# A graph attention layer: edge attributes turned by VectorE instead of TensorE, four buffers per stage instead of two, and edge lists read whole and turned into tables

## The reference, cut to what matters

```python
Q, K, V = x @ Wq + bq, x @ Wk + bk, x @ Wv + bv      # (12500, 96) each
E = edge_attr @ We + be                              # (412500, 96)
score = K[src] * Q[dst] / sqrt(12) * E               # per edge
score = exp(clip(score.reshape(-1, 8, 12).sum(-1), -5, 5))
wV = segment_sum(V[src] * score, dst)                # per destination node
Z  = segment_sum(score, dst)
out = layernorm(x + wV / (Z + 1e-6))
```

## Time and profile before

| what | value |
|---|---|
| median of 3 runs | 5354.8 us (5341.96 to 5366.8) |
| the profiled execution | 5346.04 us, its span 5344.1 us |
| TensorE's granted clock, mean | 0.508 |
| until VectorE's first product in the loop | 135.9 us |
| from VectorE's last such product (5253.25) to the end | 91 us |
| DMA packets | 497,769, 607.5 MB |

### The profile page before, as it was taken

One profiled execution on the slowest core, in us unless ns is written; L12 is line 12 of the kernel. 1 busy time (PEld: TensorE's weight loads), 2 busy tenths in 40 slices (PEclk: granted clock), 3 DMA queues, 4 the chain that ended last, 5 costly groups with the idle time before them and its releaser, 6 DMA issues.

```text
span 5344.1 us, 72613 instructions
## 1 busy us (share of the span) xinstructions
PE 3563.7 (67%) x19972; PEld 3430.0 (64%) x19973; DVE 2070.6 (39%) x6072; ACT 1676.7 (31%) x3477; POOL 3154.1 (59%) x3274
## 2 busy tenths in 40 slices
PE   7666666666666666666666666666666666666665
PEld 6666666666666666666666666666666666666664
DVE  4433333333333333333333343333333333333336
ACT  4323232333323332323332332333322323333234
POOL 4566565565665656555656566655566565665662
PEclk7555555555555555555555555555555555555555
DMA  7344444444444444444444444444444444444443
GB/s 227 107 110 118 110 109 109 109 118 110 109 111 113 115 109 110 118 110 108 110 113 113 109 108 110 114 113 109 109 110 119 108 112 112 114 109 108 110 117 91
DMA packets 497769, 607.51 MB, mean 114 GB/s; under 512 B 256053, under 2 KB 420224, under 8 KB 497630
## 3 DMA queue, kind: packets, MB, share of 16 engines
q0 software_dynamic: 155200, 318.39, 22.6%
q1 hardware_dynamic: 233215, 281.36, 18.0%
q10 hardware_dynamic: 109330, 7.48, 1.5%
HBM read 584.51 MB, written 22.46 MB: 114 GB/s over the span
## 4 chain that ended last, share of the span: by engine, by line
PE 46%; issue 25%; another core or an unknown queue 18%; DVE 6%; DVEq 2%; ACT 1%; DMA 1%; SPq 1%; ACTq 0%; POOL 0%; POOLq 0%
PE bank L637 16%; PE bank L651 15%; PE bank L635 10%; PE bank L644 4%; DVE kqe L906 2%; DVE raw_score L917 1%; DVEq L298 1%; DVE oh L901 1%; DVE kqe L898 0%; ACT eaT L767 0%; DMA out_dram<-spare 0%; ACT spare L805 0%; DVE msg L910 0%; DVE accT L925 0%
## 5 line engine op out<-in xcount | busy, mean ns | idle before, releaser
L527 POOL DMA_INDIRECT kv<-kv_table,src_idx x3224 | 3104.5, 963 | 2090.2 <-DVE msg L910 1041.2
L637 PE MATMUL bank<-w_e,eaT 97*128 97x96 f32 x6448 | 1882.9, 392 | 216.6 <-issue 216.6
L635 PE MATMUL bank<-ident,ea 128*96 128x128 f32 x3224 | 1355.3, 421 | 958.3 <-issue 517.5
L637 PEld LDWEIGHTS bank<-w_e,eaT 97*128 97x128 f32 x6448 | 1776.7, 334 | 222.8 <-issue 221.9
L898 DVE TENSOR_TENSOR kqe<-kv,bank 128x384 f32<-128x384 f32 x806 | 446.6, 554 | 3179.6 <-remote 2432.5
L651 PE MATMUL bank<-oh,msg 128*104 128x32 f32 x6448 | 1284.8, 353 | 276.7 <-issue 273.5
L635 PEld LDWEIGHTS bank<-ident,ea 128*96 128x96 f32 x3224 | 806.0, 250 | 986.2 <-issue 515.0
L651 PEld LDWEIGHTS bank<-oh,msg 128*104 128x104 f32 x6448 | 1234.3, 289 | 269.0 <-issue 264.9
L764 ACT ACTIVATE msg<-score 128x32 f32<-128x32 f32 x806 | 184.8, 229 | 3523.9 <-remote 2569.5
L644 PEld LDWEIGHTS bank<-q_win,ohT 96*128 96x128 bf16 x3224 | 401.4, 155 | 338.8 <-issue 332.4
L644 PE MATMUL bank<-q_win,ohT 96*128 96x96 bf16 x3224 | 447.2, 279 | 245.5 <-issue 241.1
(11 more groups left out here) (78 smaller groups left out, 481.0 us busy)
## 6 DMA issues: line engine op xcount, KB each, us to landing
ea<-in_edge_attr_dram SPq DMA_DIRECT2D x201, 768.0 KB
dst_b<-dst_by_chunk SPq DMA_DIRECT2D x201, 384.0 KB
kv<-kv_table,src_idx POOLq DMA_INDIRECT x3224
q_win<-q_table SPq DMA_DIRECT2D x806, 19.9 KB
kv_table<-kv_out SPq DMA_DIRECT2D x25, 336.0 KB
q_table<-q_out SPq DMA_DIRECT2D x25, 252.0 KB
spare<-in_x_dram SPq DMA_DIRECT2D x25, 168.0 KB
out_dram<-spare SPq DMA_DIRECT2D x25, 168.0 KB
```

The costliest lines, as they stand in the source:

```text
L527: pool.indirect_dma_start(kv[:, slot, g, :], None, kv_dram[:, :], bass.IndirectOffsetOnAxis(ap=src_idx[:, u, g:g + 1], axis=0)).then_inc(k ...
L635: last = nc.tensor.transpose(eaT_ps[u % 2][0:D, g * P:(g + 1) * P], ea[:, u, g, :], ident[:, :])
L637: nc.tensor.matmul(e_ps[v % 2][:, g * D:(g + 1) * D], eaT[:, v % 2, g * P:(g + 1) * P], w_e[:, :], start=True, stop=True)
```

## The change

The attributes are loaded already cut into blocks of 32 features: partition i of a block holds feature values of edges i, i+32, ... in runs of 32 floats, so that a transpose of 32x32 blocks by VectorE gives the layout that TensorE needs, features on partitions and edges along the row. TensorE turns nothing in the loop any more, and ScalarE copies nothing. The ring of loaded attributes has 16 slots of one chunk, loaded four at a time, three DMAs each, from ScalarE's queue (the first 16 from SyncE's). The PSUM banks freed by this give four buffers each of `e_ps` with `sum_ps` (which share a bank) and `q_ps`; `eaT`, `ohT`, `oh` and `msg` have four too. VectorE turns, and ScalarE builds `ohT`, four chunks ahead (`lead=DEPTH`). TensorE's step s projects chunk s, and VectorE's step a waits for TensorE's step a. The accumulation into `accT` comes five chunks late instead of three.

The edges of a chunk lie in another order (edge g*128+p at partition p, group g). The source list is read whole, made float, turned by TensorE and kept as a table, like the destinations; ScalarE copies four chunks of it at a time into `src_idx` as integers. Both lists are loaded by GpSimd instead of ScalarE. Their turning is spread over node batches 9 to 22. The inputs x are loaded by SyncE instead of ScalarE. Every second piece of `accT` is cleared by ScalarE. `x_in`, `kv_out`, `q_out` and `dst16` share memory with the loop's rings. The destination loads of the loop move from SyncE's queue to ScalarE's. The second pass is adapted in the same way.

```diff
-PROJ_LAG = 2
 SUM_LAG = 5
+DEPTH = 4
+TURN_DST = 9
+SQ = 32
 SEL = WIN * PARTS
 SEL_READ = 106
 RING = 8
 HALF = RING // 2
+EA_RING = 16
+EA_GROUP = 4
+EA_AHEAD = EA_RING - 1
...
+    for s in range(-lead, unroll):
+        step(s, s % unroll, None)
...
+        kv_mem = sb("kv_mem", [P, RING * G * 2 * D])
+        kv = kv_mem[:, :].rearrange("p (c g d) -> p c g d", g=G, d=2 * D)
+        x_in = kv_mem[:, 0:4 * BATCH * D].rearrange("p (u j d) -> p u j d", j=BATCH, d=D)
+        kv_out = kv_mem[:, 4 * BATCH * D:12 * BATCH * D].rearrange("p (u j d) -> p u j d", j=BATCH, d=2 * D)
+        ea_mem = sb("ea_mem", [P, EA_RING * CHUNK])
+        ea = ea_mem[0:D, :].rearrange("p (c e) -> p c e", e=CHUNK)
+        src_nat = ea_mem[0:NQ, 0:NJ * CHUNK]
+        dst16 = ea_mem[0:NQ, NJ * CHUNK:NJ * CHUNK * 3 // 2].bitcast(I16)
+        q_out = ea_mem[:, NJ * CHUNK * 3 // 2:NJ * CHUNK * 3 // 2 + 2 * BATCH * PARTS * D].bitcast(BF16).rearrange(
+            "p (u j k d) -> p u j k d", j=BATCH, k=PARTS, d=D)
...
-        eaT = sb("eaT", [DA, 2, CHUNK])
+        eaT = sb("eaT", [DA, DEPTH, CHUNK])
         away = sb("away", [SEL, CHUNK], BF16)
-        ohT = sb("ohT", [SEL, 2, CHUNK], BF16)
-        oh = sb("oh", [P, 2, G, WIN])
+        ohT = sb("ohT", [SEL, DEPTH, CHUNK], BF16)
+        oh = sb("oh", [P, DEPTH, G, WIN])
...
-        msg = sb("msg", [P, 2, G, DZ])
+        msg = sb("msg", [P, DEPTH, G, DZ])
...
-        eaT_ps, e_ps, q_ps, sum_ps = bank[0:2], bank[2:4], bank[4:6], bank[6:8]
+        e_ps = [bank[i][:, 0:G * D] for i in range(DEPTH)]
+        sum_ps = [bank[i][0:DZ, G * D:G * D + WIN] for i in range(DEPTH)]
+        q_ps = bank[DEPTH:2 * DEPTH]
...
+        def load_edges(engine, s, g):
+            count = min(EA_GROUP, C - s) if isinstance(s, int) else EA_GROUP
             whole = count - 1 if isinstance(s, int) and s + count == C else count
-            if whole > 0:
-                engine.dma_start(src_idx[:, u:u + whole, :], src[bass.ds(s * CHUNK, whole * CHUNK)].rearrange(
-                    "(c p g) -> p c g", p=P, g=G)).then_inc(src_idx_in[u // IDX_GROUP], 16)
-            if whole < count:
-                engine.dma_start(src_idx[:, u + whole, :], src[E - CHUNK:E].rearrange(
-                    "(p g) -> p g", g=G)).then_inc(src_idx_in[u // IDX_GROUP], 16)
+            parts = [(s * CHUNK, g * EA_GROUP, whole)] + ([(E - CHUNK, g * EA_GROUP + whole, 1)] if whole < count else [])
+            for edge, slot, chunks in parts:
+                for k in range(0, D, SQ):
+                    engine.dma_start(ea[k:k + SQ, slot:slot + chunks, :].rearrange("i c (b f) -> i (c b) f", f=SQ),
+                                     edge_attr[bass.ds(edge, chunks * CHUNK), k:k + SQ].rearrange(
+                                         "(b i) f -> i b f", i=SQ)).then_inc(ea_in[g], 16)
+        def landed_edges(engine, c, u):
+            if isinstance(c, int):
+                last = c // EA_GROUP == (C - 1) // EA_GROUP
+                engine.wait_ge(ea_in[u // EA_GROUP], 16 * (D // SQ) * (c // EA_RING + (2 if last else 1)))
+            else:
+                engine.wait_ge(ea_in[u // EA_GROUP], (c - u) * (16 * (D // SQ) // EA_RING) + 16 * (D // SQ))
...
+                if not isinstance(b, int) or 4 <= b < BATCHES:
+                    sp.wait_ge(x_turned, b - 3)
+                    load_x(sp, b, u)
+                if not isinstance(b, int) or b >= 3:
+                    m, um = b - 3, (u - 3) % 4
+                    sp.wait_ge(kv_evac, (m + 1) * 2)
+                    for lo, hi in NODE_PARTS:
+                        sp.dma_start(kv_t[lo:hi, bass.ds(m * BATCH, BATCH), :], kv_out[lo:hi, um, :, :]).then_inc(kv_stored[um], 16)
...
-                sp.wait_ge(pe_step, s - HALF + PROJ_LAG)
+                sp.wait_ge(pe_step, s - HALF)
                 sp.sem_inc(loads_allowed, 1)
-                load_edges(s, h)
-                load_destinations(s, h)
...
+            sp.wait_ge(src_turned, NJ)
+            load_edges(sp, 0, 0)
+            sp.wait_ge(dst16_stored, 32)
+            load_edges(sp, EA_GROUP, 1)
             for h in range(2):
-                load_edges(h * HALF, h)
-            sp.wait_ge(dst16_stored, 32)
-            for h in range(2):
-                load_destinations(h * HALF, h)
+                load_destinations(sp, h * HALF, h)
...
+            for g in range(2, EA_RING // EA_GROUP):
+                load_edges(sp, g * EA_GROUP, g)
...
+            for lo, hi in ((0, NP16), (NP16, NQ)):
+                pool.dma_start(dst_nat[lo:hi, :].bitcast(I32), dst[lo * NJ * CHUNK:hi * NJ * CHUNK].rearrange(
+                    "(q r) -> q r", q=hi - lo)).then_inc(dst_in, 16)
+            pool.dma_start(dst_end_row[:, :], dst[E - CHUNK:E].rearrange("(a r) -> a r", a=1)).then_inc(ends_in, 16)
+            pool.dma_start(dst_end[:, :], dst[E - CHUNK:E].rearrange("(g p) -> p g", g=G), allow_slow_non_contiguous=True).then_inc(ends_in, 16)
+            for lo, hi in ((0, NP16), (NP16, NQ)):
+                pool.dma_start(src_nat[lo:hi, :].bitcast(I32), src[lo * NJ * CHUNK:hi * NJ * CHUNK].rearrange(
+                    "(q r) -> q r", q=hi - lo)).then_inc(src_in, 16)
+            pool.dma_start(src_end[:, :], src[E - CHUNK:E].rearrange("(g p) -> p g", g=G), allow_slow_non_contiguous=True).then_inc(src_end_in, 16)
...
+            pool.wait_ge(src_in, 32)
+            nc.gpsimd.tensor_copy(src_nat, src_nat.bitcast(I32)).then_inc(src_float, 1)
...
+                j = b - TURN_DST
+                if 0 <= j < NJ:
+                    pe.wait_ge(dst_float, 1)
+                    at_least(pe, rel_made, j)
+                    turn(j, dst_nat, bank[6], dst_turned)
+                elif NJ <= j < 2 * NJ:
+                    pe.wait_ge(src_float, 1)
+                    pe.wait_ge(src_made, j - NJ + 1)
+                    turn(j - NJ, src_nat, bank[7], src_turned)
...
+                n, v, w = s - SUM_LAG, u % DEPTH, (u - SUM_LAG) % DEPTH
+                projecting = not isinstance(s, int) or s < C
+                summing = not isinstance(s, int) or n >= 0
                 if projecting:
-                    pe.wait_ge(eaT_copied, c + 1)
-                    at_least(pe, kqe_done, c - 1)
-                for g in range(G):
-                    if turning:
-                        last = nc.tensor.transpose(eaT_ps[u % 2][0:D, g * P:(g + 1) * P], ea[:, u, g, :], ident[:, :])
-                    if projecting:
-                        nc.tensor.matmul(e_ps[v % 2][:, g * D:(g + 1) * D], eaT[:, v % 2, g * P:(g + 1) * P],
+                    pe.wait_ge(ea_turned, s + 1)
+                    for g in range(G):
+                        nc.tensor.matmul(e_ps[v][:, g * D:(g + 1) * D], eaT[:, v, g * P:(g + 1) * P],
                                          w_e[:, :], start=True, stop=True)
-                if projecting:
-                    pe.wait_ge(ohT_built, c + 1)
-                    landed(pe, q_win_in, c, v, 16)
-                    sel = ohT[:, v % 2, :].rearrange("n (p g) -> n g p", g=G)
+                    pe.wait_ge(ohT_built, s + 1)
+                    landed(pe, q_win_in, s, u, 16)
                     for g in range(G):
-                        last = nc.tensor.matmul(q_ps[v % 2][:, g * D:(g + 1) * D], sel[:, g, :], q_win[0:SEL, v, :],
+                        last = nc.tensor.matmul(q_ps[v][:, g * D:(g + 1) * D], ohT[:, v, g * P:(g + 1) * P], q_win[0:SEL, u, :],
                                                 start=(g == 0), stop=(g == G - 1), skip_group_check=True)
+                else:
+                    pe.wait_ge(acc_added, n - DEPTH + 1)
+                    pe.wait_ge(msg_ready, n + 1)
                 if summing:
-                    pe.wait_ge(msg_ready, n + 1)
-                    pe.wait_ge(oh_built, n + 1)
-                    at_least(pe, acc_added, n - 1)
                     for g in range(G):
-                        last = nc.tensor.matmul(sum_ps[w % 2][0:DZ, 0:WIN], msg[:, w % 2, g, :], oh[:, w % 2, g, :],
-                                                start=(g == 0), stop=(g == G - 1))
+                        last = nc.tensor.matmul(sum_ps[v], msg[:, w, g, :], oh[:, w, g, :],
+                                                start=(g == 0), stop=(g == G - 1), skip_group_check=True)
                 last.then_inc(pe_step, 1)
...
+            def copy_sources(s, u):
+                count = max(0, min(IDX_GROUP, C - s)) if isinstance(s, int) else IDX_GROUP
+                if count > 0:
+                    nc.scalar.copy(src_idx[:, u:u + count, :], src_tab[:, bass.ds(s * G, count * G)].rearrange(
+                        "p (c g) -> p c g", g=G)).then_inc(src_copied, count)
...
+                    if u % 2 == 1:
+                        nc.scalar.copy(accT[:, bass.ds(b * (BATCH * NP), BATCH * NP)],
+                                       zero[:, 0:1].to_broadcast((P, BATCH * NP))).then_inc(acc_zeroed, 1)
...
-                c, v = s - 3, (u - 3) % RING
```

(57 more changed lines are left out.)

178 lines of the change are left out of this document (73 added, 105 removed).

## The result

| | kernel before | changed kernel |
|---|---|---|
| median | 5360.8 us (5341.96 to 5368.18, 4 runs) | 5302.79 us (5293.67 to 5312.92, 4 runs) |
| ratio | | 0.9898, 95% interval 0.9865 to 0.9931 |
| span of the profiled execution | 5344.1 us | 5300.4 us |

The forecast was 4,455 us, in a range of 4,250 to 5,200. The kernel became 1.0% faster, and the large term, the removal of 1,000 us of waits, did not come.

The account below looks back on a forecast made before the run. Gathers were taken as the floor, with some 1,000 us of waits from late TensorE signals. 141 + 10, 798 chunks x 5.20 = 4,150, 3, 91 and 50 for remaining waits, plus run offsets, gave 4,455 us, range 4,250 to 5,200.

Parts of the forecast that it names:

- the large term: Loop buffers, two to four: GpSimd never runs out of free gather buffers, so 1,000 us of waits go.
- table making: Before the loop: cast, turns, copies and moved loads delay the first free gather buffer by 10 us, ends -10 and +30.
- floor of 5.01 us: Loop: four gathers a chunk, 1.25 us from start to start, are the floor; 806 chunks give 4,038 us.
- rival 1: Loop: late signals end only when gathers pause, so longer bursts still end in 4.8 us pauses; 5,050 us, chance 0.27.
- Rival 4: Loop buffers do nothing, since signals are late by as much as buffers are deep; 5,300 to 5,400 us, chance 0.05.
- Rivals 2 and 3: Short attribute runs fill the DMA engines, 6,800 us, chance 0.06; issuing loads holds ScalarE, 6,300 us, chance 0.07.
- Transpose: VectorE gains one 96x512 transpose a chunk, 0.73 us, or 1.45 at half rate; hidden behind the gathers.
- Short runs: Attribute loads in 128-byte runs: 1.24 million packets at 14.5 ns, 17.9 ms of DMA engine time, hidden.
- ScalarE's issues: ScalarE's queue issues attribute and destination loads: 1.5 to 8 us per four chunks, hidden at 1.34 us each.
- VectorE beside the gathers: Gathers issued beside VectorE's products take 1.14 instead of 0.95 us; one in four gives 5.20 us a chunk.
- TensorE: Loop: TensorE loses four transposes a step, 4.05 to 3.50 us, both under 5.01, worth nothing by itself.

Follow-up runs that it names:

- late kind: Comparisons (series timed together) in which the unchanged kernel before took 5,361, 5,441, 5,511 and 5,326 us.
- e16: Changed kernel, loop in five stretches: gathers of 128, 64, 16 rows; plain DMAs; two of each. 4502.85 us; 6.4 us a chunk with gathers, 3.5 plain, 3.7 mixed.
- e1: Changed kernel with two buffers per stage instead of four and sums three chunks late instead of five: 5505.43 us, 1.012 of the kernel before.
- e4: Changed kernel with attributes loaded in runs of 2,048 bytes instead of 128, values in another order: 0.9856 of the kernel before.
- prompt kind: Comparisons (series timed together) in which the unchanged kernel before took 4,249, 4,260, 4,253 and 4,250 us.
- e2: Changed kernel with two gathers a chunk instead of four after the first eight chunks, half the sources left out: 3153.79 us, 3.60 us a chunk.
- e9: Changed kernel again, without an edit, beside the kernel before: 4312.28 us, 1.0124 of the kernel before.
- e10: Kernel before again, unchanged, with its profile: 4251.22 us.
- e13: Changed kernel with the x loads given back to ScalarE from SyncE: 4293.42 us, 1.0097 of the kernel before.
- e17: Changed kernel, loop in five stretches with GpSimd clearing 0, 1, 96, 192, 320 scratch columns behind each gather: 5245.01 us; 6.29, 6.34, 6.31, 6.24, 6.10 us a chunk.
- e12: Changed kernel with two buffers per stage instead of four, the edit of e1: 4317.92 us, 1.0135 of the kernel before.

## Why the prediction was wrong

**The step that failed** is the sentence "If signals come late no matter whether the gathers pause, GpSimd never runs out of free buffers and the 1,000 us of waits go." That the counts come late was read rightly. I took the lateness for a delay of fixed length, ten us, that a pause of the gathers does not change, and set four buffers of 20 us against it. The runs show that the count on which the next gathers depend comes with the pause: 3.1 us after the start of a burst's last gather before and 3.6 us after, and its lag grew with the burst, from 9.7 to 14.3 us. VectorE's waits for it stayed at 2,500 us. With four free buffers GpSimd gathers four chunks and then stands, as it stood after three or four before. The gathers of the late kind keep to a rate, 1.53 to 1.64 us each over whole loops and long stretches (1.60 before, 1.57 after), whatever their rows (e16) and however many buffers there are (e1). Depth does not bridge that. The loop takes 6.38 us a chunk before and 6.30 after, instead of 5.20. By 798 chunks the missing 1.10 us are some 875 us; the sum had allowed 50 of them, and the table making took 21 more than forecast, which together is the whole error of 848 us.

**What could have been read.** The floor of 5.01 us was taken from the shortest distance of the gathers in the earlier trace rows. The same rows give 19.73 us for a period of twelve. The row with one product and 0.92 us behind "issue", and the 1,229 us of such rows shown above, already had TensorE itself stalled. And the two microseconds between the last gather and the count were in the prediction, under rival 1.

**The rivals.** Rival 1, at a chance of 0.27, had the mechanism: late signals that end only when the gathers pause, and longer bursts that each end in a pause (5.07 us, 4.8 forecast). It let five or six chunks go by in a burst where four did, and so came to 5.8 to 6.2 us a chunk instead of 6.3. Rival 4 had the time (5,300 to 5,400) at a chance of 0.05, and half of the reason, for the lag did grow with the buffers; that they do nothing is off by the 2.2% of e1. Rivals 2 and 3 did not occur.

**The sum, term by term.** *Transpose:* 0.70 us, 0.73 taken. *Short runs:* 1.245 million packets, 1.24 forecast, and 16 x 5,300 x 0.235 by 1,245,734 is 16.0 ns each, 14.5 forecast; hidden, as e4 shows. The Trainium skill, page "DMA: Bandwidth & Descriptors", section "Specifications", asks for 512 bytes at least; by my line of two means 33 ns would have been the price of such a packet, an estimate. The trace does not bear that estimate out: 16.0 ns on the mean. *ScalarE's issues:* three attribute loads hold it 3.22 us at 3012.28; hidden. *VectorE beside the gathers:* 5.20 us a chunk taken, 5.08 where nothing else is in the way, of which the change added 0.04. *TensorE:* 3.50 us taken, 3.52 to 3.60 in e16 and e2. *Table making:* +10 forecast, +30.7 in the result (171.7 against 141.0) and +23.4 in e9 against e10. I had counted the attribute loads that pass SyncE's query stores but not the x loads: they lay in ScalarE's queue before, and in SyncE's they stand between the stores of every node batch. That is 13.4 us (e13). The remaining 10, to which the turning of both lists and the attribute loads belong, were not split further.

**The account of the result.** To the last gather 38.8 us less (5,195.0 against 5,233.8), and 4.9 less behind it: together the 43.7 us of the two spans. The loop from first freed buffer to last gather gained 69.5 and the table making gave back 30.7. In the prompt kind the loop has nothing to gain, loses 31.8 to slower gathers, and the table making 23.4 more.

**What stays open.** What it is that gathers, TensorE's and SyncE's instructions and the counts share was not found; that it is one thing is the simplest reading of e16 and e17, not shown. Whether it acts by a rate or by a least distance between gathers is open too: e17 fits neither alone. Nor is it known what makes a comparison late or prompt: neither the kernel nor its inputs differ. It is not the chip alone: the record numbers it from e1 on, and chip 4 had e1 to e4, late, and e9 to e12, prompt. The Trainium skill, page "DMA: Bandwidth & Descriptors", section "iDMA fabric — 4 AXI ports for 8 engines, asymmetric across TPBs", reports that reads of device memory by GpSimd's own DMA path slow the load stream of one core of a pair and not that of the other. The gathers here are not such reads, for they pass through the 16 DMA engines (q0, 321.69 MB), and which physical core a run had is in no record here. So no run shows it, and this is only a place to look. Why two buffers are 2.2% slower in the late kind is not settled either.

## What to carry to other kernels

Before depth is spent on a late signal, ask what ends the lateness. A delay of fixed length can be bridged by buffers; one that ends only when the other side pauses grows with them. Divide a whole period of the pattern by its work, and see whether the late engine has work in hand that it issues slowly ("issue" in gaps of equal size). If the mean distance per item stays the same when the bursts change, buffers only reshape it. In the late kind e2 and e16 show that fewer gather instructions pay, though there by leaving rows out or loading fixed ones. And a time that hangs on a contention between engines should be taken in several comparisons before an edit of 1% is kept: here the same edit was 1.0% faster in one and 1.2% slower in another.

## What the runs showed of the hardware that I had not expected

- The same program took 5,326 to 5,511 us in four comparisons and 4,249 to 4,260 in four others, at nearly the same granted clock (0.508, and 0.510 to 0.512).
- In the slower of these, indirect gathers are served at one per 1.53 to 1.64 us over long stretches, whether they move 128, 64 or 16 rows, while GpSimd issues them 1.15 to 1.51 us apart. Plain DMAs of 128 rows go out 0.53 us apart, and TensorE keeps its 3.5 us a chunk beside them (e16).
- Beside gathers that come faster, TensorE's products start 0.70 us or a multiple apart, and some of SyncE's DMA issues take 0.70 instead of 0.37 us; VectorE's and ScalarE's instructions keep their lengths.
- There, too, the count of a finished TensorE step often rises long after its last product ended (9.7 us on the median before and 14.3 after, where VectorE had to wait for it), and comes 3.1 and 3.6 us after the last gather of a burst has started. In the other kind it rises within 0.1 us behind 802 of 806 steps.
- A gather's own time on GpSimd is mostly fixed: 0.96 us for 128 rows, 0.91 for 64, 0.84 for 16 (medians in e16).
